# Filling TensorE's waits with products that nobody reads, in a four-layer AdaLN model

## The reference, cut to what matters

```
h = _layernorm(x, axis=-1) * (1 + ca) + sa
x = x + ga * attn(h, ...)
h = _layernorm(x, axis=-1) * (1 + cb) + sb
x = x + gb * ffn(h, ...)
```

## Time and profile before

| | |
|---|---|
| median of three runs | 1979.85 us |
| profiled execution: its time, its span | 1974.52 us, 1972.7 us |
| mean granted TensorE clock | 0.937 of full |
| TensorE products: busy, instructions | 1735.4 us (88%), 9347 |
| weight loads | 1383.9 us (70%) |
| VectorE, ScalarE, GpSimd busy | 1053.1, 879.0, 244.0 us |

### The profile page before, as it was taken

How to read it: one execution, slowest core, us unless ns; L and a number is a source line. 1 busy time by engine, 2 the same in 40 slices (tenths; PEclk the granted TensorE clock), 3 DMA queues, 4 the chain that set the end, 5 groups by cost and what they waited for, 6 DMA issues and landing times. The chain is left out here.

```text
span 1972.7 us, 27425 instructions
## 1 busy us (share of the span) xinstructions
PE 1735.4 (88%) x9347; PEld 1383.9 (70%) x9347; DVE 1053.1 (53%) x2115; ACT 879.0 (45%) x1706; POOL 244.0 (12%) x237
## 2 busy tenths in 40 slices
PE   4989787997779999999887887997999999999898
PEld 4767645674658888888662676875788888888755
DVE  2265525334345555555547434546666766667466
ACT  3466524333334444444466543436544544444334
POOL 2001002110112222222200111221000000000000
PEclk9899896998779999999898997998999999999799
DMA  3000030110023333333200013321000000000100
GB/s 102 11 11 16 0 128 9 32 40 0 18 73 112 112 112 112 112 112 112 83 1 0 33 32 82 112 82 46 3 15 16 16 16 11 4 16 0 42 0 21
DMA packets 47075, 91.50 MB, mean 46 GB/s; under 512 B 7697, under 2 KB 24081, under 8 KB 46810
## 3 DMA queue, kind: packets, MB, share of 16 engines
q1 hardware_dynamic: 47026, 90.89, 15.2%
HBM read 89.52 MB, written 1.35 MB: 46 GB/s over the span
## 5 line engine op out<-in xcount | busy, mean ns | idle before, releaser
L438 PE MATMUL bank<-l1m_src_hi,l1m_w_hi 128*128 128x512 f32 x384 | 150.2, 391 | 7.4 <-DVE l1m_src_lo L507 7.4
L438 PE MATMUL bank<-l1m_src_lo,l1m_w_hi 128*128 128x512 f32 x384 | 150.0, 391 | 0.0
L438 PE MATMUL bank<-l1m_src_hi,l1m_w_lo 128*128 128x512 f32 x384 | 149.9, 390 | 0.0
L2251 ACT ACTIVATE l_mem<-bank 128x129 f32<-128x129 f32 x240 | 64.6, 279 | 185.9 <-PE bank L2101 185.1
L410 POOL TENSOR_TENSOR l1m_w_lo<-l1m_w,l1m_w_hi 128x512 fp32r<-128x512 f32 x96 | 104.7, 1109 | 325.5 <-ACT l1m_w_hi L475 325.5
L514 DVE TENSOR_TENSOR l1m_a<-l1m_s,bank 128x512 f32<-128x512 f32 x96 | 66.0, 687 | 116.2 <-ACT l1m_s L487 116.2
L491 ACT ACTIVATE l1m_a_hi<-l1m_a 128x512 fp32r<-128x512 f32 x96 | 60.7, 633 | 146.6 <-DVE l1m_a L520 146.6
L528 DVE TENSOR_TENSOR l1m_a_lo<-l1m_a,l1m_a_hi 128x512 fp32r<-128x512 f32 x96 | 66.5, 692 | 70.9 <-ACT l1m_a_hi L491 70.9
L2101 PE MATMUL bank<-l_dr,l_nkt 128*128 128x129 f32 x480 | 99.2, 309 | 2.9 <-DVE l_dr L2401 2.0
L2398 DVE RECIPROCAL l_inv<-bank 128x1 f32<-128x1 f32 x240 | 38.9, 162 | 109.8 <-PE bank L2111 109.0
L487 ACT ACTIVATE l1m_s<-bank 128x512 f32<-128x512 f32 x96 | 57.4, 598 | 87.6 <-PE bank L438 87.6
(11 more groups left out here) (537 smaller groups left out, 4366.4 us busy)
## 6 DMA issues: line engine op xcount, KB each, us to landing
l1m_w<-in_l1f_win SPq DMA_DIRECT2D x48, 256.0 KB, 2.9
l1m_wr<-l1f_token_weights SPq DMA_DIRECT2D x32, 384.0 KB, 3.4
l1m_wr<-l1f_token_weights SPq DMA_DIRECT2D x32, 256.0 KB, 3.8
l_w<-in_l_w SPq DMA_DIRECT2D x9, 768.0 KB, 4.4
wmod<-in_wmod SPq DMA_DIRECT2D x4, 1536.0 KB, 10.3
l1m_w<-in_l1f_wout SPq DMA_DIRECT2D x48, 128.0 KB, 3.0
l1m_wr<-l1f_token_weights SPq DMA_DIRECT2D x32, 128.0 KB, 3.1
l2e_wr<-l2f_token_weights SPq DMA_DIRECT2D x16, 256.0 KB, 3.8
```

Of the source, the lines that this page charges most:

```text
L438: last = pe.matmul(k.bank[:, 2 * c + part, :], wq[:, half, at:at + P], xq[:, b, chunk(c)], start=(b == 0 and q == 0), stop=(b == DB - 1 an ...
L2251: act.activation(mem[:, a, (n + 1) % 2, 0:W1], k.bank[:, MEM + a, 0:W1], ACT.Identity).then_inc(s["mem_copied"], 1)
```

## The change

`Core` gets a method that issues `count` products of the identity with the tile of zeros, 128x512 in f32, each with `start=True, stop=True`, into one bank. They carry no semaphore and nothing reads them. It is called in seven places: three products behind the variances of every norm (bank 7), two behind the last products of `gated_units` (bank 0), and one at the end of layer 0's, 1's and 3's attention parts and behind the output projection of layer 2's (bank 7, for layer 1 bank 0).

```diff
+    def idle_products(self, pe, count, bank=7):
+        for _ in range(count):
+            pe.matmul(self.bank[:, bank, :], self.ident[:], self.zeros[:], start=True, stop=True)
...
@@ LayerNorm.on_tensor
             last.then_inc(s["var_ready"], 1)
+        k.idle_products(pe, 3)
@@ gated_units
                 down(pairs, -2)
                 down(pairs, -1)
+                k.idle_products(pe, 2, 0)
@@ l0_attention
                         last.then_inc(y_ready, 1)
+                k.idle_products(pe, 1)
@@ l1_attention
                     last.then_inc(s["y_ready"], 1)
+                k.idle_products(pe, 1, 0)
```

## The result

The changed kernel takes 1966.14 us (median of 4 runs, 1964.77 to 1966.87); the kernel before took 1978.96 us beside it. The ratio is 0.9941, 95% interval 0.9921 to 0.9961. So it is 12.8 us faster (7.7 to 15.6 by the interval) where 22.8 us were forecast: inside the range of 1946 to 1969 us, at the upper end of the likeliest case's own spread, 1949 to 1967.

The account below looks back on a forecast made before the run. TensorE's work and waits were taken to set the time, with about 249 us at half clock. Gains of 13.8 (norms), 7.5 (short series) and 1.5 (dense work) make 22.8 us: 1979.85 to 1957 us, range 1946 to 1969.

Parts of the forecast that it names:

- likeliest case: Whole kernel: the forecast of 1957 us, given a chance of 0.57, with its own spread of about 1949 to 1967.
- Sum (a): Norms: if each starts at full clock, five save 1.69 us each and two slow ones 2.72 and 2.59, together 13.8 us.
- Sum (b): Five short series behind norms, 29.3 us together: a later fall of the clock wins at most 11.3 us, 7.5 taken.
- Sum (c): Dense work behind norms that ran at half clock, 22.1 us: at most 11.1 us won, 1.5 us taken.
- The step from one profile to the median: Whole kernel: the profiled execution was 5.3 us faster than the median run; this was carried over unchanged, 1979.85 - 22.8.
- Zeros do not count: Added products: multiplying zeros by an identity prevents no fall of the clock, 1980 us; chance 0.09.
- Only the norms gain: Short series and dense work behind norms: the clock still falls early and they give nothing; norms alone give 1966 us; chance 0.20.
- The clock never falls near norms: Norms, short series and dense work all gain in full, 36.2 us, giving 1944 us; chance 0.09.
- Late products: Behind norms: added products at half clock outlast the wait and delay following work by 13.5 us, 1993 us; chance 0.05.
- at least seven of nine norms at 7.15 us: Trace sign: at least seven of the nine norm stretches after the first norm take 7.15 us at clock 1.00.
- series of 3.6 to 5 us: Trace sign: the short series behind norms should take 3.6 to 5 us each; 5.5 us would show the forecast wrong.
- The rule on transposes: Skill page: identity transposes do not engage full clock; the prediction held that the trace disagrees; if right for products, 1980 us.

Follow-up runs that it names:

- the cut: GpSimd's w_lo subtraction in layer 2 split, two thirds moved behind the inner norm, against the kernel with three products at gated ends; 1954.3 us.

## Why the prediction came out as it did

**Sum (a), the norms: 13.8 us taken, 6.0 us found.** This is the step that was off most. Of the seven slow norms three were saved, for 1.69 + 2.59 + 1.69 us. Three kept 8.84 us because two products leave 2.0 to 2.2 us idle at a gated end, and I wrote "I take all of it; the lower end is half, if waits of 1.9 us still let the clock fall now and then". The lower end, 6.9 us, was near the truth. The trace had the warning: at 2.39 us the clock fell, at 1.74 us it did not the earlier trace rows, and the slow norm at 1852.32 stood behind a wait of 1.90 us, just the length that two products were to leave:

```profile
1852.32 5.38 PE L257 MATMUL bank<-x_stream,mean_w 128*128 128x256 f32 x16 [1.90 <-PEq L88]
```

A third product removes the falls (1.1 to 1.3 us idle, 7.15 us in every such norm), and 7.9 us of time with them. What decides near 2 us was not found: 1.90 us lost the clock here and 1.95 us kept it at 1321.18, so the length of the wait is not all of it. The seventh, the norm inside layer 2's attention part, reached full clock, but none of its 2.72 us reached the end: the path there runs over GpSimd, which holds VectorE's multiplication until its own instruction ends. I costed that norm from TensorE's window alone and did not ask who waits for its end.

**Sum (b), the short series: 7.5 us taken, 5.2 us found.** 5.59, 5.37, 3.79, 5.47 and 3.97 us are 24.2 us instead of 29.3. The mechanism is right, the fall is delayed and not abolished, and the bound of 18.0 us for all five at full clock is confirmed by the 3.63 us with six products. What was wrong is to count them as independent of (a). In the profiles with three or four products, series of 4 or 8 columns behind a stage's end take 5.1 to 5.5 us where the norm ahead had lost the clock (5.37, 5.47 in the changed kernel) and 3.7 to 4.5 us where it had kept it (3.97; 3.89 and 4.08 with the third product); L1873's in the two kernels with filled waits is the exception, 5.5 us. The series with 64 columns took 3.79 us either way. And not all of it reached the end. At L2556 the series became 3.03 us faster and the norm ahead of it 1.69 us, but L2602 starts only 2.03 us sooner behind the norm's first mean (35.55 instead of 37.58 us): L2575 now waits 2.07 us for VectorE's `l3f_ea`, and the clock falls once more behind it. The same step in the kernel before, where L2602 is L2590:

```profile
1889.90 0.47 PE L2590 MATMUL bank<-l3f_h_hi,l3f_pick 128*128 128x512 f32 x1 [3.38 <-DVE l3f_val L2726]
```

**Sum (c), dense work: 1.5 us taken.** Behind L667 the half clock went from 6.11 to 2.95 us, behind L2556 from 5.46 to 2.95 us, at L2062 from 3.92 to 2.94 us; behind the other norms it stayed at 3.4 to 3.9 us. Half of the differences is 1.6 + 1.3 + 0.5 us, and the 1.3 were lost in the wait above. What reached the end, 2.1 us, is near the 1.5.

**The step from one profile to the median.** I took the profile's 5.3 us below the median as spread over the waits ("this one got away at 277.37, 1088.12 and L974"). A second execution shows that 277.37 and 1088.12 repeat at full clock, and that L974 was the one that got away: it opens the one stretch in which the two differ, layer 0's feed-forward part. The sums hold nothing for it, since the profile had it at full clock. The changed kernel's profile was less lucky there (161.61 us), so the two profiles differ by 8.7 us and the medians by 12.8. Against the second profile of before the difference is 13.8 us in the spans: 6.0 of the norms, 3.3 in that stretch, and 4.5 for the rest, the series and the dense work above all. The 164.9 us go with the fall at L974; what decides between 158.6 and 161.6 us was not found.

**The rivals.** "Zeros do not count" is refuted by the products of data. "Only the norms gain" has the right number and the wrong way: the kernel with slow norms behind every end and products behind them has 10.4 of the 12.8 us. "The clock never falls near norms" was not reached even with six products and the long waits filled (1951.6 us at best). "Late products" did not occur, since every norm ended at full clock. Where lateness was forced, 13.2 us of it cost 3.6; but those products ran at full clock and the rival's would not, so its price of 13.5 us stays untested.

**The signs.** Of the signs named ahead of the result, at least seven of nine norms at 7.15 us and series of 3.6 to 5 us did not come: five norms took 7.15 us, three still showed 0.81, and three of the five series took 5.4 to 5.6 us. The mean clock of 0.946 instead of 0.948 and the unchanged start behind the variances did.

**The rule on transposes.** In the changed kernel the transposes L1447 are alone on TensorE from about 548.4 to 551.9 us, and the clock goes from 0.50 to full in their last half microsecond (0.68 is the mean of that slice), before TensorE's next product at 553.01:

```profile
548.28 3.62 PE L1447 MATMUL bank<-ident,l1f_w 128*64 128x128 f32 x16
553.01 1.07 PE L1453 MATMUL bank<-l1f_wt,ident 64*64 64x512 f32 x2 [1.11 <-ACT l1f_wt L1465]
```

```profile
549.50:550.50 1.00, 1.00 (x7) 0.82 (x6) 0.83 (x6) 0.26 (x1) 0.00 (x0) 0.50 0.00 0
552.50:553.50 1.00, 0.49 (x2) 0.19 (x3) 0.00 (x0) 0.46 (x1) 0.00 (x0) 1.00 0.00 0
551.50:552.00 0.50, 0.41 (x2) 0.00 (x0) 0.00 (x0) 0.06 (x1) 0.00 (x0) 0.68 0.00 0
```

This repeats. The Trainium skill, "TensorE: Matmul & The Clock Gate", Part 4, says that transposes do not engage the full clock. This trace disagrees for these transposes in f32. The added products are products by an identity and not transposes; that they hold the clock says nothing for or against the page.

## What to carry to other kernels

Work that nobody reads, put into a wait that cannot be shortened, is free as long as it ends before the wait does, and it can pay more than its length by holding TensorE's clock: the third product, 0.86 us at each of four places, was worth 7.9 us. Size it by the idle time that it leaves, and try one product more before stopping (at the ends of stages here, 1.9 to 2.2 us left lost the clock in four places of five, 1.5 us or less kept it in all). Look also at what follows a norm or series that gets faster: the clock can fall there instead. Follow each saved microsecond to the next wait: where another engine's chain ends last, as at the inner norm and at layer 3's selection, it is not saved. And profile the same kernel twice before comparing stage by stage, since a single stretch can carry half the difference.

## What the runs showed of the hardware

- GpSimd and VectorE: a `scalar_tensor_tensor` with two inputs in SBUF that takes 0.47 us took 2.73 us when a GpSimd `tensor_tensor` of 6.71 us was under way, and ended 0.3 us behind it; `tensor_tensor` with one input in PSUM (L278) was not delayed (0.69 us each during the same GpSimd instruction). The Trainium skill, "SBUF — State Buffer", section "SBUF: two separate sides", describes the pair of ports that both engines share as an exclusive lock that the first takes for a whole instruction. The traces agree: the delayed instruction ended 0.3 us behind GpSimd's in the kernels before and after. With the cut, a longer one (1.28 us elsewhere) took 5.50 us and ended 1.1 us behind.
- Products of zeros hold TensorE's clock like products of data (1966.14 and 1964.53 us, the same norms slow).
- Series of 32 instructions with 4 to 64 columns never raised the clock and often lost it, although TensorE was busy without a gap: wholly at half clock they take 7.00 us (8 columns), wholly at full clock 3.63 us.
- Between identical executions most falls of the clock repeat (nine norms within 0.05 us), and a few do not: behind one wait of 3.47 us the clock held in one profile of the kernel before (3.70 us for the next eight instructions) and fell in the other (5.40 us), and the stretch took 158.64 us in the one and 164.95 us in the other.
- How long TensorE idles does not alone decide whether the clock falls at the next work: 1.95 us kept it at one place (after), 1.90 us lost it at another (before).
